# Gate logits of a fused attention and mixture-of-experts layer: fp16 halves of the transposed norm rows in place of their fp32 copy

## The reference

```python
x = x + attention(ln(x), ctx, ctx) @ Wfc.T + bfc        # 32 query heads, 8 key/value groups, width 16
h = ln(x)
logits = h @ gate_weight.T                              # 2048 x 8, float32
scores = softmax(logits)
# the two best of four groups of two experts, then the two best experts in them
routed = sum over the two experts e: score_e * (silu(h @ gate_w[e].T) * (h @ up_w[e].T)) @ down_w[e].T
shared = (silu(h @ sh_gate_w.T) * (h @ sh_up_w.T)) @ sh_down_w.T
x = x + routed + shared
```

## Time and profile before

| | us |
|---|---|
| median of 3 runs | 754.7 |
| lowest and highest | 753.55, 754.98 |
| the profiled execution's own time | 754.92 |
| its span | 753.1 |

### The profile page before, as it was taken

How to read it: one execution, slowest core, us unless ns; L and a number is a source line. 1 busy time by engine, 2 the same in 40 slices (tenths; PEclk the granted TensorE clock), 3 DMA queues, 4 the chain that set the end, 5 groups by cost and what they waited for, 6 DMA issues and landing times.

```text
span 753.1 us, 16125 instructions
## 1 busy us (share of the span) xinstructions
PE 732.2 (97%) x5325; PEld 398.9 (53%) x5326; DVE 561.1 (75%) x1191; ACT 419.0 (56%) x845; POOL 272.1 (36%) x221
## 2 busy tenths in 40 slices
PE   6998999999999999999999999999999999999998
PEld 3554533434444334656665566555555556655554
DVE  4777689999999967788589998655555555546776
ACT  3667468888888884777543454343433334223222
POOL 3264006999997311664400401212111121016540
PEclk9999999999999999999999999999999999999999
DMA  9898946755755798997578664977767779549993
GB/s 328 332 409 282 252 147 187 221 168 176 220 150 151 249 344 301 345 386 281 190 204 259 153 155 123 197 175 181 184 168 184 173 180 213 127 124 283 329 308 92
DMA packets 155100, 168.17 MB, mean 223 GB/s; under 512 B 97952, under 2 KB 111776, under 8 KB 154528
## 3 DMA queue, kind: packets, MB, share of 16 engines
q1 hardware_dynamic: 143724, 126.20, 57.6%
q0 software_dynamic: 10720, 40.12, 17.0%
q10 hardware_dynamic: 596, 1.07, 0.4%
HBM read 104.09 MB, written 41.42 MB: 193 GB/s over the span
## 4 chain that ended last, share of the span: by engine, by line
PE 53%; DVE 23%; DMA 8%; issue 6%; POOL 4%; ACT 3%; SPq 2%; DVEq 0%; POOLq 0%; ACTq 0%
PE psum L1521 21%; DVE sb_rows L1786 12%; PE psum L1538 11%; PE psum L1523 4%; PE psum L1448 4%; PE psum L1257 4%; POOL sb_weights L952 4%; DMA sb_weights<-k_parts 2%; DMA sb_weights<-in_wdn 2%; PE psum L1540 2%; PE psum L1233 1%; DVE sb_rows L1915 1%; PE psum L1281 1%; DMA x_dram<-sb_rows 1%; DMA sb_rows<-xb_dram 1%
## 5 line engine op out<-in xcount | busy, mean ns | idle before, releaser
L1521 PE MATMUL psum<-sb_weights,sb_rows 128*128 128x352 f16 (+1 forms) x1344 | 209.7, 313 | 0.0
L1521 PEld LDWEIGHTS psum<-sb_weights,sb_rows 128*128 128x128 f16 x1344 | 131.2, 98 | 76.1 <-issue 1.2
L1786 DVE TENSOR_REDUCE sb_rows<-psum 128x4 f32<-128x1024 f32 x128 | 150.0, 1214 | 4.6 <-PE psum L1281 4.5
L1073 ACT ACTIVATE sb_weights<-psum 128x512 f32<-128x512 f32 x256 | 139.4, 595 | 22.8 <-PE psum L1353 19.7
L1538 PE MATMUL psum<-sb_weights,sb_hT 128*128 128x512 f16 (+1 forms) x522 | 122.2, 379 | 0.0
L1147 ACT ACTIVATE psum<-psum 128x352 f32<-128x352 f32 x68 | 30.5, 448 | 124.9 <-DVE psum L2040 112.3
L933 POOL DMA_INDIRECT sb_rows<-xn_rows,sb_slot_tok x36 | 34.6, 960 | 176.7 <-DVE sb_rows L2418 134.8
L1353 PE MATMUL psum<-sb_weights 50*128 50x512 f16 x256 | 86.6, 387 | 1.7 <-ACT sb_weights L1073 0.9
L1367 PE MATMUL psum<-sb_weights 128*32 128x256 f32 x1024 | 82.6, 394 | 0.3
L1538 PEld LDWEIGHTS psum<-sb_weights,sb_hT 128*128 128x128 f16 x522 | 50.9, 98 | 54.0 <-issue 0.6
L1281 PE MATMUL psum<-sb_weights 48*128 48x256 f16 x512 | 70.7, 274 | 1.6 <-DMA sb_weights<-k_parts 0.9
(11 more groups left out here) (307 smaller groups left out, 1172.8 us busy)
## 6 DMA issues: line engine op xcount, KB each, us to landing
sb_weights<-in_wgu SPq DMA_DIRECT2D x20, 704.0 KB, 7.1
sb_weights<-in_wgu POOLq DMA_DIRECT2D x20, 704.0 KB, 6.8
sb_weights<-in_wdn SPq DMA_DIRECT2D x17, 768.0 KB, 6.3
slot_y<-sb_rows SPq DMA_DIRECT2D x36, 256.0 KB, 2.4
sb_weights<-q_parts SPq DMA_DIRECT2D x96, 64.0 KB, 3.0
x_dram<-sb_rows SPq DMA_DIRECT2D x24, 256.0 KB, 4.6
q_parts<-sb_weights SPq DMA_DIRECT2D x16, 256.0 KB, 4.1
sb_rows<-in_x POOLq DMA_DIRECT2D x16, 256.0 KB, 5.8
```

What stands on the lines that cost most here:

```text
L1073: nc.scalar.activation(probs[G % 2][:, kt, pair * 512:(pair + 1) * 512], bank[4 + f % 2], ACT.Exp, scale=exp_by[n]).then_inc(exp_done, 1)
L1521: mm = nc.tensor.matmul(to[:, 0:F], x_T[:, at:at + P], gu(wp, k, which), start=first, stop=last)
L1786: nc.vector.tensor_reduce(to[:, :, j // UB, :, j % UB, qt], psum[:, banks[qt] * 512:(banks[qt] + 2) * 512] .rearrange("p (a h k) -> p a h ...
```

## The change

The fp32 copy `lnT` and its evacuation (L1085) go. The gate weight is scaled by a power of two and cut into two fp16 halves, once. Each gate is then eight fp16 products instead of four fp32 ones: for each of four blocks of features the high and the low half of the rows are the weights in turn, and both halves of the gate weight move side by side (16 columns). So the high halves' and low halves' products land in two groups of 8 columns, which are evacuated with the inverse scale into two planes and added once for all tokens at the head of the routing.

```diff
@@ ScalarE
-                nc.scalar.activation(ln16[s][:, 0:D], bank[4 + s][:], ACT.Copy, scale=X_SCALE)
-                nc.scalar.copy(lnT[s], bank[4 + s][:]).then_inc(lnt_evac, 1)
+                nc.scalar.activation(ln16[s][:, 0:D], bank[4 + s][:], ACT.Copy, scale=X_SCALE).then_inc(lnt_evac, 1)
@@ gate_out
-                nc.scalar.copy(logits[:, bass.ds(t, 1), :], bank[6 + s][:, 0:NE].unsqueeze(1)).then_inc(gate_evac, 1)
+                nc.scalar.activation(route[:, 0:2, bass.ds(t, 1), :],
+                                     bank[6 + s][:, 0:2 * NE].rearrange("p (s e) -> p s e", s=2).unsqueeze(2), ACT.Copy,
+                                     scale=dn_inv[:, NE + SH:DN_TOPS]).then_inc(gate_evac, 1)
@@ TensorE, gate(t, s)
-                pe.wait_ge(lnt_evac, t + 1)
+                pe.wait_ge(ln16_done, t + 1)
...
                 for k in range(KD):
-                    mm = nc.tensor.matmul(bank[6 + s][:, 0:NE], lnT[s][:, k * P:(k + 1) * P], gw_sb[:, k, :],
-                                          start=(k == 0), stop=(k == KD - 1))
+                    for part in range(2):
+                        at = part * D + k * P
+                        mm = nc.tensor.matmul(bank[6 + s][:, 0:2 * NE], ln16[s][:, at:at + P],
+                                              gw16[:, k].rearrange("p s e -> p (s e)"),
+                                              start=(k == 0 and part == 0), stop=(k == KD - 1 and part == 1))
...
                 if t == 3:
+                    pe.wait_ge(scale_done, 5)
                     gate(0, 0)
@@ VectorE, attention
+                if G == 3:
+                    dve.wait_ge(w_fc, 48)
+                    nc.vector.tensor_reduce(dn_max[:, NE + SH:DN_TOPS], gw_sb[:].rearrange("p k e -> p (k e)"), AX.X, ALU.max,
+                                            apply_absolute_value=True)
@@ VectorE, token stage
+            def gate_halves():
+                g = slice(NE + SH, DN_TOPS)
+                dve.wait_ge(scale_done, 2)
+                nc.vector.tensor_scalar(dn_inv_i[:, g], dn_inv_i[:, g], float(10 << 23), None, ALU.subtract).then_inc(scale_done, 1)
+                nc.vector.tensor_scalar(gw16[:, :, 0, :], gw_sb[:], dn_scale[:, g], None, ALU.mult).then_inc(scale_done, 1)
+                dve.wait_ge(scale_done, 4)
+                nc.vector.scalar_tensor_tensor(gw16[:, :, 1, :], gw_sb[:], dn_scale[:, g], gw16[:, :, 0, :],
+                                               ALU.mult, ALU.subtract).then_inc(scale_done, 1)
...
                 residual_norm(t, t % 2, t // 2)
+                if t == 2:
+                    gate_halves()
@@ softmax_in
                 dve.wait_ge(gate_evac, TILES)
+                link(nc.vector.tensor_tensor(logits, logits, score, ALU.add))
                 link(nc.vector.tensor_reduce(t_tile[:, 0, :], logits, AX.X, ALU.max))
```

More of the change, by code:

```diff
@@ L81 @@
 CUT_W = 8
+DN_TOPS = NE + SH + 1
 PA, PB, PC = SH * EARLY, SLOTS, SH * (TILES - EARLY)
@@ L223, in build @@
         a_in += [dn_tail[:], bfc_sb]
[L224 to L228, removed]
+        dn_max = sb("dn_max", [P, DN_TOPS])
+        dn_max_all = sb("dn_max_all", [DN_TOPS, 1])
+        dn_exp = sb("dn_exp", [P, DN_TOPS], I32)
+        dn_scale_i = sb("dn_scale_i", [P, DN_TOPS], I32)
+        dn_inv_i = sb("dn_inv_i", [P, DN_TOPS], I32)
         dn_scale, dn_inv = dn_scale_i[:].bitcast(F32), dn_inv_i[:].bitcast(F32)
@@ L276, in build @@
         res_in, x2_sb, xn2_sb = [row(0), row(1)], [row(2), row(3)], [row(4), row(5)]
-        lnT = [row(6), row(7)]
-        xb_sb = lnT
+        xb_sb = [row(6), row(7)]
         ln16 = [zero_row[:].bitcast(F16), ln16_sb[:].bitcast(F16)]
-        w_max_rows = row(6)[0:NE + SH, 0:P]
+        w_max_rows = row(6)[0:DN_TOPS, 0:P]
         tok_in, xT, mid, late = [row(0), row(1)], [row(2), row(3)], [row(4), row(5)], [row(6), row(7)]
@@ L305, in build @@
         wsel = sb("wsel", [P, TILES, NE])
+        gw16 = wsel[:].rearrange("p t e -> p (t e)")[:, 0:KD * NE].bitcast(F16).rearrange("p (k s e) -> p k s e", k=KD, s=2)
         sel = sb("sel", [P, TILES, NE])
@@ L1481, in _ @@
                     pe.wait_ge(dn_max_done, NE + SH)
-                    nc.tensor.transpose(bank[5][0:NE + SH, 0:P], dn_max[:], ident[:]).then_inc(w_max_t, 1)
+                    nc.tensor.transpose(bank[5][0:DN_TOPS, 0:P], dn_max[:], ident[:]).then_inc(w_max_t, 1)
                 else:
                     pe.wait_ge(w_max_b, 2)
-                    nc.tensor.transpose(bank[5][:, P:P + NE + SH], w_max_rows,
-                                        ident[0:NE + SH, 0:NE + SH]).then_inc(w_max_tt, 1)
+                    nc.tensor.transpose(bank[5][:, P:P + DN_TOPS], w_max_rows,
+                                        ident[0:DN_TOPS, 0:DN_TOPS]).then_inc(w_max_tt, 1)
             for t in range(2, 4):
@@ L1999, in down_scales @@
                 dve.wait_ge(w_max_tt, 2)
-                link(nc.vector.tensor_scalar(dn_max[:], bank[5][:, P:P + NE + SH], 2.0 ** -100, None, ALU.max))
+                link(nc.vector.tensor_scalar(dn_max[:], bank[5][:, P:P + DN_TOPS], 2.0 ** -100, None, ALU.max))
                 link(nc.vector.tensor_scalar(dn_exp[:], dn_max[:].bitcast(I32), 0x7F800000, None, ALU.bitwise_and))
@@ L2004, in down_scales @@
                                         ALU.subtract).then_inc(scale_done, 1)
+            def gate_halves():
[6 more added lines that the diff above has]
+                                               ALU.mult, ALU.subtract).then_inc(scale_done, 1)
             residual_norm(0, 0, 0)
             dve.wait_ge(w_max_t, 2)
-            nc.vector.tensor_reduce(dn_max_all[:], bank[5][0:NE + SH, 0:P], AX.X, ALU.max).then_inc(w_max_b0, 1)
+            nc.vector.tensor_reduce(dn_max_all[:], bank[5][0:DN_TOPS, 0:P], AX.X, ALU.max).then_inc(w_max_b0, 1)
             dve.wait_ge(w_max_b0, 2)
-            nc.vector.tensor_copy(w_max_rows, dn_max_all[:].broadcast_to([NE + SH, P])).then_inc(w_max_b, 1)
+            nc.vector.tensor_copy(w_max_rows, dn_max_all[:].broadcast_to([DN_TOPS, P])).then_inc(w_max_b, 1)
             residual_norm(1, 1, 0)
```

## The result

| | before | after |
|---|---|---|
| median, us | 753.93 (17 executions, 750.62 to 755.52) | 756.19 (17 executions, 752.66 to 760.78) |
| ratio, 95% interval | | 1.0035 (1.0022 to 1.0049) |
| profiled execution: time, span, mean granted clock | 754.92, 753.1, 0.998 | 757.02, 755.2, 0.993 |

What follows compares the result with a forecast made beforehand. TensorE, busy for 97% of the span, was taken as the bound. Gains of 2.7 us by stretch less 0.45 added make 2.25: 752.7 against the profiled 754.92, 752.4 for the median, range 749.2 to 754.7.

Steps and rivals of the forecast that it cites:

- The gate on TensorE: Token stage: eight fp16 products at 25.6 ns take 0.20 us where the gate took 0.81, a gain of 0.61 per gate.
- (2) gate_halves: VectorE behind tile 2's norm: cutting the gate weight costs some 0.6 us, hidden by 1.05 us of idle time.
- (3): Each gate's wait for cut_rows: the cut is done before TensorE arrives; only at the last gate within 0.2 us.
- The sum by stretch: Token stage in four stretches: gains of 0, 0.5, 1.1 and 1.1 us, together 2.7, bounds 0.8 and 7.2.
- The third stretch: 349.17 to 364.38 us: 0.61 of one gate plus 0.48 of the loop, gain 1.1 us, bounds 0.5 and 2.4.
- the tail: 364.38 to 376.47 us, the fourth stretch: 0.48 for L1085 plus 0.61 for the last gate, gain 1.1, bounds 0.3 and 1.7.
- the first two stretches: 301.28 to 349.17 us: gain 0 in the first, pinned by DMAs, and 0.5 us in the second, loop 0.48 shorter.
- DMAs and late adds take everything back: Rival: before 364 us nothing is won, only the last stretch counts, 1.1 - 0.45 = 0.65: 754.1 us. Chance 0.18.
- What is added: Costs of new work: 0.15 us for the reduction and 0.3 for the sum of planes, 0.45 together; the others 0 or hidden.
- The reduction: Attention, 32 columns: 0.15 us added, bounds 0 and 0.2; its wait for the gate weight costs nothing.
- The sum of planes: Head of the routing, VectorE: one operation on 128x128 elements, 0.3 us added, at least 0.
- The chance of slower: Rival: narrow products on TensorE don't overlap, 0.178 us each, 7.3 us more over some 12 gates: 762.0. Chance 0.04.

Runs made afterwards that it cites:

- e2: Kernel after, with gate_halves right behind the scales, ahead of the norm of tile 2: 754.51 us, ratio 1.0014.
- e4: Kernel after, with 17 identity transposes on TensorE ahead of gate 0's wait and 17 ahead of gate 13; the waits stay: 754.38 us, ratio 1.0015.
- e1: Kernel after, with gate 13 behind the first shared product and its evacuation one place later on ScalarE: 755.84 us, ratio 1.0033.
- e12: e9's kernel measured again, on the chip of e8 and e10: 751.25 us, ratio 0.9979.
- e8: e3 with the first silu ahead of gate 13's evacuation and without TensorE's wait for gate 14's evacuation: 751.8 us, ratio 0.9977.
- e3: Kernel after, with both the moves of e1 and e2: 752.84 us, ratio 0.9994.
- e10: e8 with SyncE's load of the transposed rows ahead of the two stores in steps 14 and 15: 751.54 us, ratio 0.9976.
- e7: e3 with the dropped fp32 evacuation put back on ScalarE, its result unused: 755.21 us, ratio 1.0016.
- e5: e3 with ScalarE's first part of the expert weight ahead of the standard deviation: 755.19 us, ratio 1.0019.
- e9: e10 with ScalarE's first part moved as in e5: 751.29 us, ratio 0.9959.

## Why the prediction was wrong

**The gate on TensorE: right.** 0.20 to 0.21 us from a gate to what follows, as the distance of 25.6 ns said. The eight products take 0.18 us where the chain lists them; the Trainium skill's rule for weight loads (TensorE: Matmul & The Clock Gate, LDWEIGHTS), 107 ns for 128 columns, would have made 0.85, an estimate. The trace disagrees with it.

**"(2) gate_halves ... That hides it": the first step that failed.** I took three operations of 0.17 us from small operations on one SBUF input or on PSUM, and asked only whether VectorE had 1.05 us to spare there. I didn't ask what GpSimd does there: in the trace before, its scaling runs from 300.81 to 303.34, over that very idle time. L2023 reads two SBUF operands, and took 2.40 us under GpSimd's operation, 0.25 without (e2). "The first gate waits for it by 0.1 to 0.2 us" became 2.05. The rows needed were in the trace before: L2019, of the same form, took 1.79 us where GpSimd's operation (325.12 to 327.98) overlapped it by 0.31 us, and 2.64 where it (335.55 to 338.41) overlapped by 1.16. Both end 1.48 us behind GpSimd. GpSimd's timeline before:

```profile
300.81 2.53 POOL L838 TENSOR_TENSOR sb_weights<-sb_weights,sb_w_scale_i 128x1408 f32<-128x1408 f32 x1 [10.09 <-ACT sb_weights L1119]
...
325.12 2.86 POOL L848 TENSOR_TENSOR sb_weights<-sb_weights 128x1408 f16<-128x1408 f32 x1
...
335.55 2.86 POOL L848 TENSOR_TENSOR sb_weights<-sb_weights 128x1408 f16<-128x1408 f32 x1
```

I took them as a spread of lengths and didn't look for its cause. The Trainium skill (SBUF — State Buffer, section SBUF: two separate sides) states it: VectorE and GpSimd share a pair of SBUF ports, and a VectorE operation with two SBUF inputs and a GpSimd one that reads SBUF hold it in turn, whichever starts first, for its whole instruction. The trace agrees: 2.40 us, ending within 0.04 us of GpSimd's instruction.

**"(3) ... so it finds it done": the second.** In the loop, `gate(t-3)` stands behind `out_project(t)`, and the cut of its tile was in `residual_norm(t-1)`: there was never a wait. Behind the loop the order is another: `gate(13)` follows `gate(12)` directly, and its cut is part of `residual_norm(15)`, which starts when `out_project(15)` has ended. TensorE therefore waits for an add, the statistics and a cut, 365.00 to 367.68 us: 2.53 us, where I had put nothing. I carried the loop's distance over to the unrolled end and looked there at the last gate alone ("the gates of tiles 12 to 14 ... count for nothing").

**The clock: a term I hadn't.** The earlier trace rows shows 1.00 everywhere, and I wrote "always"; but in that execution TensorE had no hole over 0.5 us in the stage. The trace before also held a fall: after two microseconds (102 to 104) in which TensorE was busy for 0.39 and 0.70 us, the granted clock was 0.71 from 105 to 106 and 0.50 from 106 to 108. Two holes of 2.05 and 2.53 us brought the lower level, and slowed what came behind by 0.8 us (`out_project`), 0.9 (the transposes behind gate 0) and 1.5 (the shared product). e4 puts both together at about 1.5 us of the median. Whether the stage keeps 1.00 in every execution of the kernel before isn't shown: 50 of the 102 beside the runs of e1 to e12 have a mean clock of at most 0.995, below the profiled one's 0.998.

**The sum by stretch: right behind the tenth add, unproven ahead of it.** The third stretch gave 1.05 for 1.1, in every changed kernel that left it alone, and the tail 1.26 for 1.1 once its own new wait was gone (e8). For the first two stretches I had 0.5. e3 gave 0.60, but the same program gave -0.70, -1.12 and -0.27 in e2, e8 and e10, so that hit is luck and no gain is shown there. I had the pace of stretch two from the loop over L1085 (9.54 us), and e7 shows that it isn't: the second part grows until it ends 1.5 us behind GpSimd, and the loop over a load of rows is about as long. The rival "DMAs and late adds take everything back" is true there, if not of stretch three. The medians of e8, e10 and e12 come near the total of 2.25 us (0.9977, 0.9976 and 0.9979 for 0.9970), but only with gates, a wait and an order changed that the forecast didn't know of. And the forecast's inner range, 751.0 to 753.9, is not half of the way to its bounds: those are 754.3 and 748.0 by its sum, and half of the way is 753.4 and 750.2.

**What is added: right elsewhere.** The reduction: the two row maxima around it start 1.23 us apart, where two in a row take 1.13 (2.35 - 1.22), so 0.10 for the 0.15 I took (timelines of VectorE before and after). The sum of planes takes 0.27 us and cost nothing, where I took 0.3: from the third shared product to the routing's matmul it is 50.14 us in both traces (376.32 to 426.46; 378.12 to 428.26). The wait of 0.5 that I expected there didn't appear.

**The chance of slower, 0.04**, hung on a single mechanism, the price of a product, for which the earlier trace rows left no room. I had listed the new waits under "what would make it wrong" ("TensorE waiting for `cut_rows`") and given them no price.

## What to carry to other kernels

When a change makes an instruction wait for something new, find its place in each of its calls, the unrolled ones ahead of and behind the loop too, and name the step there that produces what it waits for. Before a gain on one engine is counted, write down the length of every loop that closes over the same tiles: here TensorE's, the one over GpSimd and the one over a load were 10.4 to 10.5 us long, and the last as long as its load. And before a hit in one stretch is believed, see whether a second execution repeats it. And where the engine that sets the pace has had no hole yet, price a new one twice: its length, and the slower clock behind it.

## What the runs showed of the hardware that I had not expected

- A VectorE operation with two SBUF inputs on 128x32 elements took 2.40 us while GpSimd worked, ending with GpSimd's instruction, and 0.25 us without. With 128x1408 elements: 1.68 us alone, up to 3.62 with GpSimd.
- A hole of 1.5 to 2.5 us in TensorE's work can bring the granted clock from 1.00 to 0.50 (2.4 to 1.2 GHz), but doesn't in every execution: 2.05 and 2.53 us did in the kernel after, 2.53 in e2, 1.71 in e5, two close together of 1.33 and 1.55 in e9, 1.70 did in e3 and not in e1, and 1.92 didn't in e1. Short transposes in the hole kept it at 1.00 in the execution profiled (e4).
- Of the 17 executions of the kernel after, the two at a mean clock of 1.000 took 752.66 and 754.35 us, and those at 0.993 or less 756.23 to 760.78. So a part of the spread of one kernel is how often the clock fell.
